# A Mamba-2 layer with a linear side branch: y_diag in channel-major form, split fp32r output projection, x times dt out of PSUM, and new instruction orders

## The chip, the cores and the metric

The kernel runs on one core of a Trainium2 chip. The core has a matmul engine (TensorE, in the profile PE, with its weight loads as PEld), a vector engine (VectorE, DVE), an activation engine (ScalarE, ACT), a general engine (GpSimd, POOL) and SyncE (SP), which issues the DMAs here. SBUF is the on-chip memory, PSUM holds matmul results in eight banks of 512 fp32 columns. The metric is the device time of one execution in microseconds (us). Before the change it is 858.38 us, the median of three runs (854.18 to 859.85).

## The reference

Two sequences of 4096 tokens and 256 features go through one layer. Cut to what matters:

```python
xn = layernorm(x)                                   # no gain or bias
zxbcdt = xn @ W_in                                  # 256 -> 512 z | 768 xBC | 8 dt
z, xBC, dt = split(zxbcdt)
dt = softplus(dt + dt_bias)                         # 8 heads
xBC = silu(causal_conv(xBC, conv_w) + conv_b)       # 4 taps per channel
xs, B, C = split(xBC)                               # 512 | 128 | 128
y = ssd(xs * dt, dt * a, B, C)                      # state-space recurrence, heads of 64
y = (y + xs * D) * silu(z)
y = y * rsqrt(mean(y * y) + EPS) * rms_w
h = xn + y @ W_out
attn = layernorm(h) * ln_g + ln_b
ffn = tanh(xn @ weight @ aux_weight1 @ aux_weight2 + bias)
out = x + attn + ffn
```

The recurrence is computed chunk by chunk: within a chunk, y_diag[l] = sum over s <= l of (C[l].B[s]) exp(A_cum[l] - A_cum[s]) (x dt)[s]; from the chunks before, y_off[l] = exp(A_cum[l]) C[l] . state; then state = decay * state + B^T (x dt weights).

## The kernel before

**Tiling.** A step is a chunk of 128 tokens of both sequences (q = 0, 1), so there are 32 steps. The four engines each run `one_pass(k, b)` for k from -2 to 33, and one pass works on pieces of up to four steps: a pass does the norm statistics of step k+2, the projections of k+1 and k, the recurrence of k and k-1 and the output of k-2. Nothing schedules this at run time: in each engine's `one_pass` the calls stand in the order in which they are issued, and semaphores between the engines hold an instruction until its inputs are there. Buffers of three steps rotate.

**A step on its way.** `norm_stats`, `norm_mean_var` and `norm_apply` (DVE, with a pow on POOL) make xn; `transpose_x` (PE) puts it into a PSUM bank with channels on partitions; ACT's `high_part` rounds it to fp32r and DVE's `low_part` keeps the remainder, so that each projection can be three fp32r products (high x high, high x low, low x high) in place of one fp32 one. `branch_project` makes the side branch and dt in the two banks ring0 and ring1, which ACT's `branch` reads one after the other (tanh, relu, abs); `softplus_exp` (ACT) and then the DVE steps `softplus(k, b, i)` make dt and, as the last one, a_wide = dt * a. These are 11 small instructions (16 columns, the last 64), of which each needs the one before. `conv_project` (six blocks of 128 channels) is followed by `conv_in` (ACT: bias and last tap) and three `tap` instructions of DVE per block, each of which adds to what the tap before wrote. `conv_silu` and `z_silu` (ACT) finish xs and gate.

**The recurrence.** `sums` (PE) makes the cumulated sums of a_wide; ACT copies their rows, DVE's `low_rows` and POOL's `spread_rows` make the operands of one fp32r matmul per four heads, `exponents`, whose result ACT's `decay` takes the exponential of. `b_and_g` makes C.B, `mask_g` (POOL) masks it, `weigh` (DVE) multiplies it with the decays into mm. `x_tokens` transposes xs to tokens on partitions (PE) and ACT copies it to SBUF as xsb; from xsb ACT makes xdt with eight instructions of 64 columns, POOL makes xw (state weights) and xd (skip, x * D). `y_diag` is then eight fp32 matmuls, one per head, with mm[128x128] stationary and xdt of 64 columns moving:

```python
last = mul(yd_bank[:, h * HD:(h + 1) * HD], mm[:, q, h], xdt[:, q, h * HD:(h + 1) * HD], ...)
```

**The output.** `scale_off` (DVE) scales y_off, `add_skip` (POOL) adds xd, `add_diag` and `apply_gate` (DVE) give yg. `square` (ACT) sums its squares, `rms_scale` (POOL, two small instructions per sequence, one of them a pow) makes rr. `transpose_y` and `y_channels` bring yg to channels on partitions, `out_project` is four fp32 matmuls of 256 columns, `last_h` (DVE) applies rr and adds xn. `last_stats`, `last_mean_var`, `last_norm_scale` (POOL, three small instructions per sequence), `last_apply` (ACT) and `output` (POOL) end the step, for each sequence by itself.

**Banks and what follows from them.** yd_bank holds in turn y_diag and the transposed yg of each sequence: `y_diag` of one waits until `y_channels` has read the other's. yoff_bank is shared by `y_off` and `out_project`, xt_bank by `x_tokens` and `states`. A conv or z projection waits until the taps or silu that read its ring bank are through.

## Time and profile before

| | |
|---|---|
| runs, median (lowest to highest) | 858.38 us (854.18 to 859.85) |
| profiled execution | 857.2 us, span 855.5 us |
| granted TensorE clock, mean | 0.976 |
| busy in the span: PE, DVE, POOL, ACT | 800.8, 726.5, 702.0, 681.3 us |
| chain that ended last, largest lines | DVE taps 7%, POOL xw 7%, PE conv and branch products 5% |
| DMA | 19.98 MB, 23 GB/s, hardly busy after the first slice |

The span is the time from the first to the last instruction, and the execution is 1.7 us longer. The first 50 us and the last 55 us are set-up, filling and draining of the pipeline; between them every engine repeats its pass. On PE a matmul in fp32 stands as two records, and PE counts as busy until a modelled end, so its cost is read from start to start. Instructions of DVE and ACT that do not need each other overlap: the next one starts before the last has ended.

### The profile page before, as it was taken

What the parts mean: (1) busy time and instruction counts of PE and PEld (TensorE: products, weight loads), DVE (VectorE), ACT (ScalarE), POOL (GpSimd) and SP (SyncE); (2) the same over time, 40 slices, a digit from 0 to 9 for tenths busy, and PEclk for the clock granted to TensorE, in tenths of its full rate; (3) what the DMA queues carried; (4) which work ended last, traced back from release to release, by engine and by line L of the source; (5) the groups of instructions that cost most, each with busy time, mean ns of one, the idle gap of its engine ahead of it and who ended that gap; (6) DMA issues with size and microseconds to landing.
All of it is one profiled execution on the core that took longest, in us unless ns stands there. A gap on an engine that the chain in (4) does not pass through costs nothing.

```text
span 855.5 us, 18389 instructions
## 1 busy us (share of the span) xinstructions
PE 800.8 (94%) x4944; PEld 671.5 (78%) x4944; DVE 726.5 (85%) x1826; ACT 681.3 (80%) x1767; POOL 702.0 (82%) x1096
## 2 busy tenths in 40 slices
PE   1479999999999999999999999999999999999974
PEld 1368888888888888888888888888888888888753
DVE  1669899998999999899999999999999998998741
ACT  1169888898888888988888889888888898888841
POOL 4036888898888889988888899888888988888884
PEclk9689999999999999999999999999999999999986
DMA  5000000000000000000000000000000000000000
GB/s 174 0 1 13 14 26 26 26 11 14 25 25 25 25 25 25 6 19 25 25 25 25 25 25 1 24 25 25 25 25 25 25 0 24 25 25 13 14 13 25
DMA packets 20848, 19.98 MB, mean 23 GB/s; under 512 B 2646, under 2 KB 20568, under 8 KB 20824
## 3 DMA queue, kind: packets, MB, share of 16 engines
q1 hardware_dynamic: 20824, 19.71, 7.2%
q8 instruction: 10, 0.16, 0.1%
q14 instruction: 14, 0.11, 0.0%
HBM read 11.31 MB, written 8.39 MB: 23 GB/s over the span
## 4 chain that ended last, share of the span: by engine, by line
POOL 39%; DVE 25%; issue 17%; PE 13%; ACT 2%; SPq 2%; POOLq 1%; DVEq 1%; DMA 0%; ACTq 0%
DVE u L624 7%; POOL xw L446 7%; PE ring L1012 5%; POOL obuf L491 4%; POOL left L434 3%; POOL sdec L453 3%; POOL xd L461 3%; POOL rs L483 3%; DVE pa L646 3%; POOL right L430 3%; DVE lay L677 3%; POOL obuf L493 3%; POOL btg L441 2%; DVE lay L683 2%; PE yoff_bank L1149 2%
## 5 line engine op out<-in xcount | busy, mean ns | idle before, releaser
L624 DVE SCALAR_TENSOR_TENSOR u<-ring,cw,u 128x256 f32<-128x256 f32 x576 | 260.5, 469 | 30.4 <-ACT u L847 29.8
L1012 PE MATMUL ring<-xhl,wh 128*128 128x262 f32 x768 | 174.8, 319 | 3.4 <-DVE u L624 3.4
L1012 PE MATMUL ring<-wh,xhl 128*128 128x512 f32 (+1 forms) x512 | 164.1, 374 | 3.3 <-DVE u L624 3.3
L1012 PEld LDWEIGHTS ring<-xhl,wh 128*128 128x128 f32 x768 | 124.7, 193 | 43.6 <-DVE u L624 21.6
L847 ACT ACTIVATE u<-ring,cb,cw 128x256 f32<-128x256 f32 x192 | 107.9, 562 | 45.6 <-PE ring L1012 40.9
L907 ACT ACTIVATE xdt<-xsb,dts 128x64 f32<-128x64 f32 x512 | 128.5, 335 | 0.0
L1131 PE MATMUL yd_bank<-xdt,lay 128*128 128x64 f32 x1024 | 123.2, 274 | 0.9 <-ACT yts L916 0.9
L1149 PE MATMUL yoff_bank<-wo,yts 128*128 128x256 f32 x512 | 122.1, 382 | 1.1 <-ACT yts L916 0.7
L1131 PEld LDWEIGHTS yd_bank<-xdt,lay 128*128 128x128 f32 x1024 | 121.2, 194 | 1.7 <-ACT yts L916 1.3
L1012 PE MATMUL ring<-xhl,wl 128*128 128x262 f32 x384 | 110.2, 287 | 0.0
L1012 PEld LDWEIGHTS ring<-wh,xhl 128*128 128x128 f32 x512 | 93.9, 192 | 20.0 <-issue 7.2
L1149 PEld LDWEIGHTS yoff_bank<-wo,yts 128*128 128x128 f32 x512 | 93.9, 192 | 13.9 <-issue 2.7
L860 ACT ACTIVATE xs<-u 128x512 f32<-128x512 f32 x96 | 60.2, 627 | 45.8 <-DVE u L624 45.5
L677 DVE SCALAR_TENSOR_TENSOR lay<-e_bank,btg 128x512 f32<-128x512 f32 x128 | 86.7, 678 | 1.3 <-POOL btg L441 0.4
L1012 PE MATMUL ring<-wl,xhl 128*128 128x264 f32 (+1 forms) x256 | 87.8, 343 | 0.0
L467 POOL TENSOR_TENSOR lay<-lay,xd 128x512 f32<-128x512 f32 x64 | 81.6, 1276 | 0.0
L891 ACT ACTIVATE e_bank<-e_bank 128x512 f32<-128x512 f32 x128 | 75.4, 590 | 0.3
L1012 PEld LDWEIGHTS ring<-xhl,wl 128*128 128x128 f32 x384 | 73.6, 192 | 0.0
L1112 PE MATMUL yoff_bank<-state,xs 128*128 128x512 f32 x128 | 68.4, 616 | 1.6 <-DVE hh L705 1.3
L491 POOL TENSOR_TENSOR obuf<-hh,lng 128x256 f32<-128x256 f32 x64 | 46.5, 727 | 28.4 <-ACT hh L897 28.4
L705 DVE SCALAR_TENSOR_TENSOR hh<-yoff_bank,rr,xn 128x256 f32<-128x256 f32 x64 | 30.5, 477 | 44.8 <-POOL rr L474 38.4
L1100 PE MATMUL e_bank<-right,left 128*128 128x512 f32 x128 | 66.6, 522 | 1.4 <-POOL left L434 1.4
(134 smaller groups left out, 1995.7 us busy)
## 6 DMA issues: line engine op xcount, KB each, us to landing
xin<-in_x_dram SPq DMA_DIRECT2D x32, 256.0 KB, 2.9
out_dram<-obuf SPq DMA_DIRECT2D x32, 256.0 KB, 2.8
lay<-in_w_in_dram SPq DMA_DIRECT2D x1, 1288.0 KB
wo<-in_w_out_dram SPq DMA_DIRECT2D x1, 512.0 KB
lay<-in_f1t_dram SPq DMA_DIRECT2D x1, 256.0 KB
lay<-in_f2t_dram SPq DMA_DIRECT2D x1, 256.0 KB
lay<-in_f_dram SPq DMA_DIRECT2D x1, 256.0 KB
lng<-in_ln_g_dram SPq DMA_DIRECT2D x1, 128.0 KB
```

Of the source, the lines that this page charges most:

```text
L467: g.tensor_tensor(t2[:, q], t1[:, q], xd[:, q], ALU.add).then_inc(t2_done[q], 1)
L491: g.tensor_tensor(obuf[:, b, q], hh[:, q], lng[:, :], ALU.mult).then_inc(hg_done[q], 1)
L624: v.scalar_tensor_tensor(out=u[:, ct], in0=conv_bank(ct)[:, :, t:t + P], scalar=cw[:, ct, t:t + 1], in1=u[:, ct], op0=ALU.mult, op1=ALU.ad ...
L677: v.scalar_tensor_tensor(out=mm[:, q, hs], in0=e_bank[half][:, :].rearrange("p (j t) -> p j t", t=P), scalar=1.0, in1=btg[:, q, P:2 * P].u ...
L847: s.activation(u[:, ct], conv_bank(ct)[:, :, HALO:PH], ACT.Identity, bias=cb[:, ct:ct + 1], scale=cw[:, ct, HALO:TAPS]).then_inc(u_done[ct ...
L891: s.activation(e_bank[half][:, :], e_bank[half][:, :], ACT.Exp).then_inc(e_done[q][half], 1)
L907: last = s.activation(xdt[:, q, head], xsb[:, q, head], ACT.Copy, scale=dts[:, b, q * H + h:q * H + h + 1])
L1012: last = mul(out, a, c, start=first and i == 0, stop=i == n - 1)
L1100: mul(bank[:, :], left[:, 2 * q + half], right[:, :, :].rearrange("p j t -> p (j t)"), start=True, stop=True)\
L1112: mul(yoff_bank[:, :], xs[:, b, KI + 1, q], state[:, q], start=True, stop=True).then_inc(yoff_in_psum[q], 1)
L1131: last = mul(yd_bank[:, h * HD:(h + 1) * HD], mm[:, q, h], xdt[:, q, h * HD:(h + 1) * HD], start=True, stop=True)
L1149: last = mul(yoff_bank[:, 0:D], yts[:, q, ki], wo[:, ki], start=ki == 0, stop=ki == KI - 1)
```

## The change

1. `LOG_TERMS` goes from 6 to 5: one softplus instruction less per step.
2. ring0 and ring1 become one tensor of two banks, and `branch` reads both with three instructions in place of six.
3. `out_project` uses the three-product form: W_out is split at the start into woh and wol, ACT rounds the transposed yg to fp32r (yts), a new DVE instruction `y_low` keeps the remainder (ytl), and 12 fp32r matmuls take the place of four fp32 ones.
4. `y_diag` is swapped: xdt (64 columns) is stationary, mm (128) moves, the result has channels on partitions, two heads above each other. A new ACT copy `y_copy` takes it to SBUF, `add_skip` adds the skip there (which `skip_x` now makes from xs directly), and a new `y_tokens` transposes it back (4 transposes). `add_diag` adds t1.
5. x times dt is read from PSUM; the copy xsb is gone, xw is made from xdt, and w16 is gone.
6. EPS of the rms norm comes in as a constant 513th column of yg, and `rms_scale`, `last_norm_scale` and `output` do both sequences at once.
7. The four orders are new. `exponents` is one matmul per four heads before and after.

The heart of the diff (orders left out):

```diff
-LOG_TERMS = 6
+LOG_TERMS = 5
...
-        ring0, ring1, e_bank0, e_bank1, xt_bank, bg_bank, yoff_bank, yd_bank = [
+        ring = ctx.enter_context(nc.psum_tensor("ring", [P, 2, 512], F32))
+        ring0, ring1 = ring[:, 0], ring[:, 1]
+        e_bank0, e_bank1, xt_bank, bg_bank, yoff_bank, yd_bank = [
...
-            def scale_x(k, q):
-                pool.wait_ge(xsb_done[q], k + 1)
-                pool.wait_ge(w16_done, k + 1)
-                g.tensor_tensor(heads(xw[:, q]), heads(xsb[:, q]), per_head(w16[:, q * H:(q + 1) * H]), ALU.mult)\
+            def scale_x(k, b, q):
+                pool.wait_ge(xdt_done[q], k + 1)
+                pool.wait_ge(sums_read, k + 1)
+                if begun(k - 1):
+                    pool.wait_ge(st_in_psum[q], k)
+                g.tensor_tensor(heads(xw[:, q]), heads(xdt[:, q]), per_head(exs[:, b, Q * H + q * H:Q * H + (q + 1) * H]), ALU.mult)\
...
             def add_skip(k, q):
-                pool.wait_ge(t1_done[q], k + 1)
+                pool.wait_ge(yc_done[q], k + 1)
                 pool.wait_ge(xd_done[q], k + 1)
-                g.tensor_tensor(t2[:, q], t1[:, q], xd[:, q], ALU.add).then_inc(t2_done[q], 1)
...
+                g.tensor_tensor(yct[:, q], yct[:, q], xd[:, q], ALU.add).then_inc(t2_done[q], 1)
...
+            def rms_scale(k):
+                pool.wait_ge(ss_done[0], k + 1)
+                pool.wait_ge(ss_done[1], k + 1)
...
+                g.tensor_tensor(rr[:, :], ss[:, :], nhalf[:, :], ALU.pow).then_inc(rr_done, 1)
...
+            def output(k, b):
+                pool.wait_ge(hn_done[0], k + 1)
+                pool.wait_ge(hn_done[1], k + 1)
                 pool.wait_ge(stored[b], count16(k, b))
...
+                both = [P, Q, D]
+                g.tensor_tensor(obuf[:, b], hh[:, :, :], lng[:, :].unsqueeze(1).to_broadcast(both), ALU.mult).then_inc(hg_done, 1)
+                pool.wait_ge(hg_done, k + 1)
+                g.tensor_tensor(obuf[:, b], obuf[:, b], res[:, b], ALU.add).then_inc(out_done, 1)
...
             for ki in range(KI):
-                v.tensor_scalar(wo[:, ki], wo[:, ki], rmsw[:, ki:ki + 1], None, ALU.mult)
+                last = v.tensor_scalar(woh[:, ki], wo[:, ki], rmsw[:, ki:ki + 1], None, ALU.mult)
+            last.then_inc(s_sel, 1)
+            dve.wait_ge(s_sel, 11)
+            for ki in range(KI):
+                v.scalar_tensor_tensor(out=wol[:, ki], in0=wo[:, ki], scalar=rmsw[:, ki:ki + 1], in1=woh[:, ki].bitcast(F32),
+                                       op0=ALU.mult, op1=ALU.subtract)
...
+            def y_low(k, q):
+                dve.wait_ge(yts_done[q], k + 1)
+                bank = yd_bank[:, :].rearrange("p (k t) -> p k t", k=KI)
+                v.tensor_tensor(ytl[:, q], bank, yts[:, q].bitcast(F32), ALU.subtract).then_inc(ytl_done[q], 1)
...
-            def branch(k, q):
-                act.wait_ge(f_in_psum[q], k + 1)
-                bank = (ring0, ring1)[q]
+            def branch(k):
+                act.wait_ge(f_in_psum[0], k + 1)
+                act.wait_ge(f_in_psum[1], k + 1)
...
-                    last = s.activation(xdt[:, q, head], xsb[:, q, head], ACT.Copy, scale=dts[:, b, q * H + h:q * H + h + 1])
+                    last = s.activation(xdt[:, q, head], xt_bank[:, head], ACT.Copy, scale=dts[:, b, q * H + h:q * H + h + 1])
...
+            def y_copy(k, q):
+                act.wait_ge(yc_in_psum[q], k + 1)
+                if begun(k - 1):
+                    act.wait_ge(yd_in_psum[q], k)
+                s.activation(yct[:, q], yd_bank[:, :], ACT.Copy).then_inc(yc_done[q], 1)
...
             def y_diag(k, q):
                 if begun(k - 1 + q):
-                    pe.wait_ge(yts_done[1 - q], k + q)
+                    pe.wait_ge(ytl_done[1 - q], k + q)
...
-                    last = mul(yd_bank[:, h * HD:(h + 1) * HD], mm[:, q, h], xdt[:, q, h * HD:(h + 1) * HD],
+                    half = slice(h % 2 * HD, (h % 2 + 1) * HD)
+                    last = mul(yd_bank[half, h // 2 * P:(h // 2 + 1) * P], xdt[:, q, h * HD:(h + 1) * HD], mm[:, q, h],
                                start=True, stop=True)
+                last.then_inc(yc_in_psum[q], 1)
+
+            def y_tokens(k, q):
+                pe.wait_ge(t2_done[q], k + 1)
+                for ki in range(KI):
+                    last = tr(yd_bank[:, ki * P:(ki + 1) * P], yct[:, q, ki * P:(ki + 1) * P], ident[:, :])
                 last.then_inc(yd_in_psum[q], 1)
...
             def out_project(k, q):
-                pe.wait_ge(yts_done[q], k + 1)
+                pe.wait_ge(ytl_done[q], k + 1)
...
+                pairs = []
                 for ki in range(KI):
-                    last = mul(yoff_bank[:, 0:D], yts[:, q, ki], wo[:, ki], start=ki == 0, stop=ki == KI - 1)
+                    pairs += [(yts[:, q, ki], woh[:, ki]), (yts[:, q, ki], wol[:, ki]), (ytl[:, q, ki], woh[:, ki])]
+                last = split_products(yoff_bank[:, 0:D], pairs)
```

**DVE around the softplus steps.** On DVE, before, a stretch in which the first two blocks of taps (L624, u) of step k+1 are done, with the first softplus steps den, rc and sv between them; the ISA and REGISTER_ALU rows only count semaphore values:

```order
L624 SCALAR_TENSOR_TENSOR u<-ring,cw,u 128x256
L637 SCALAR_TENSOR_TENSOR den<-ee 128x16
L623 ISA
L624 SCALAR_TENSOR_TENSOR u<-ring,cw,u 128x256 x2
L623 REGISTER_ALU
L624 SCALAR_TENSOR_TENSOR u<-ring,cw,u 128x256
L635 ISA
L640 RECIPROCAL rc<-den 128x16
L624 SCALAR_TENSOR_TENSOR u<-ring,cw,u 128x256
L635 REGISTER_ALU
L642 TENSOR_TENSOR sv<-ee,rc 128x16
L624 SCALAR_TENSOR_TENSOR u<-ring,cw,u 128x256
```

The same steps in the change, from y_low (L716) and new_state (L702) of step k-1 on:

```order
L716 TENSOR_TENSOR ytl<-yd_bank,yts 128x512
L702 TENSOR_TENSOR state<-xt_bank,sdec 128x512
L649 SCALAR_TENSOR_TENSOR den<-ee 128x16
L647 ISA
L652 RECIPROCAL rc<-den 128x16
L647 REGISTER_ALU
L654 TENSOR_TENSOR sv<-ee,rc 128x16
L647 REGISTER_ALU
L656 TENSOR_TENSOR ww<-sv 128x16
L647 REGISTER_ALU
L658 SCALAR_TENSOR_TENSOR pa<-ww 128x16
L647 REGISTER_ALU
```

They go on without anything between them to a_wide (ten steps in all); the taps, which shared the stretch, follow them, six in a row for blocks 2 and 0 (and as many for blocks 4 and 5 later), each block's three behind each other.

**PE around y_diag of sequence 0.** Before, behind the transposes of xn (L1005) and ahead of sums of the next step (L1069 to L1071):

```order
L1100 MATMUL e_bank<-right,left 128x512
L999 REGISTER_ALU
L1005 MATMUL ring<-ident,xn 128x128 x4
L1131 MATMUL yd_bank<-xdt,lay 128x64 x8
L1069 MATMUL bg_bank<-a_wide,upto 128x16
L1070 MATMUL bg_bank<-a_wide,after 128x16
L1071 MATMUL bg_bank<-upto,a_wide 128x128
```

In the change it stands between two conv projections (L1024), ahead of the transposes of xs (L1093) of the next step and the first products of the output projection of the sequence before:

```order
L1024 MATMUL ring<-xhl,wl 128x262
L1144 MATMUL yd_bank<-lay,xdt 64x128 x8
L1024 MATMUL ring<-xhl,wh 128x262 x2
L1024 MATMUL ring<-xhl,wl 128x262
L1024 MATMUL ring<-xhl,wh 128x262 x2
L1024 MATMUL ring<-xhl,wl 128x262
L1093 MATMUL xt_bank<-ident,xs 128x128 x4
L1024 MATMUL yoff_bank<-woh,yts 128x256
L1024 MATMUL yoff_bank<-wol,yts 128x256
```

Its output is now 64 partitions by 128 columns per head, and it has moved away from sums, which now open PE's pass and wait there for a_wide.

**POOL behind mask_g.** The change's POOL in the middle of its pass: the bias of res (L417), last_norm_scale for both sequences (L487 to L497), add_skip of sequence 1 (L472), the output of both (L504, L506) and scale_x (L450):

```order
L417 TENSOR_TENSOR res<-res,lnb 128x512
L487 TENSOR_SCALAR ve<-mv 128x2
L492 TENSOR_SCALAR shift<-mv 128x2
L494 TENSOR_TENSOR rs<-ve,nhalf 128x2
L497 TENSOR_TENSOR shift<-shift,rs 128x2
L472 TENSOR_TENSOR yct<-yct,xd 128x512
L502 ISA
L504 TENSOR_TENSOR obuf<-hh,lng 128x512
L506 TENSOR_TENSOR obuf<-obuf,res 128x512
L450 TENSOR_TENSOR xw<-xdt,exs 128x512
```

Before, the same place held residual's bias and then sequence 1's own small chain:

```order
L410 TENSOR_TENSOR res<-res,lnb 128x512
L472 TENSOR_SCALAR sse<-ss 128x1
L474 TENSOR_TENSOR rr<-sse,nhalf 128x1
L461 TENSOR_TENSOR xd<-xsb,d_bc 128x512
L467 TENSOR_TENSOR lay<-lay,xd 128x512
L479 TENSOR_SCALAR ve<-mv 128x1
L483 TENSOR_TENSOR rs<-ve,nhalf 128x1
```

The wide output instructions and the add of the skip now stand together, behind a wait for y_copy.

## Rows read from the trace of the kernel before

**Rows 1.** Windows, 400 to 600 us: length, busy us (count) per engine, clock, DMA.

```profile
400.00:600.00 200.00, 199.92 (x1256) 168.01 (x1256) 183.22 (x458) 172.32 (x451) 177.17 (x271) 1.00 0.07 21
```

**Rows 2.** Timeline of DVE (start us, duration us): a_wide of steps 2 and 31.

```profile
98.63 0.22 DVE L659 TENSOR_TENSOR a_wide<-dts,a_neg 128x64 f32<-128x64 f32 x1
...
806.99 0.21 DVE L659 TENSOR_TENSOR a_wide<-dts,a_neg 128x64 f32<-128x64 f32 x1
```

**Rows 3.** Chain that ended last, 795 to 856 us: start, us, records of PE.

```profile
794.94 1.51 PE yoff_bank L1149 x7
...
796.78 1.38 PE ring L1012 x6
...
800.44 0.44 PE xt_bank L1081 x4
800.88 0.73 PE ring L1012 x6
...
827.07 0.86 PE yoff_bank L1112 x2
...
828.17 1.75 PE yd_bank L1131 x16
```

**Rows 4.** Waits: who for whom, us in total, times, longest.

```profile
DVE hh L705 <- POOL rr L474: 38.4, 30, 3.0
```

**Rows 5.** Timeline of DVE: instructions that do not need each other.

```profile
407.17 0.48 DVE L624 SCALAR_TENSOR_TENSOR u<-ring,cw,u 128x256 f32<-128x256 f32 x1
407.56 0.68 DVE L677 SCALAR_TENSOR_TENSOR lay<-e_bank,btg 128x512 f32<-128x512 f32 x1
408.16 0.68 DVE L683 TENSOR_TENSOR lay<-yoff_bank,exs 128x512 f32<-128x512 f32 x1
```

**Rows 6.** Groups by form, ACT: shapes xcount | busy us, mean ns | idle before.

```profile
L879 ACT ACTIVATE xsb<-xt_bank 128x512 f32<-128x512 f32 x64 | 40.0, 625 | 2.2 <-PE xt_bank L1081 2.2
...
L912 ACT ACTIVATE junk<-lay 128x512 f32<-128x512 f32 x64 | 39.5, 617 | 0.4 <-DVE lay L698 0.4
```

**Rows 7.** Timeline of DVE: instructions that need the one before.

```profile
53.96 0.17 DVE L650 SCALAR_TENSOR_TENSOR pb<-pa,sv 128x16 f32<-128x16 f32 x1
54.16 0.17 DVE L653 SCALAR_TENSOR_TENSOR dts<-pb,relu 128x16 f32<-128x16 f32 x1
...
808.68 0.70 DVE L694 TENSOR_TENSOR yd_bank<-yd_bank,lay 128x512 f32<-128x512 f32 x1 [1.48 <-PE yd_bank L1131]
809.42 0.69 DVE L698 TENSOR_TENSOR lay<-yd_bank,gate 128x512 f32<-128x512 f32 x1
```

**Rows 8.** Timeline of all engines, 424 to 450 us: pa on DVE beside POOL.

```profile
433.92 1.27 POOL L410 TENSOR_TENSOR res<-res,lnb 128x512 f32<-128x512 f32 x1
434.27 0.96 DVE L646 SCALAR_TENSOR_TENSOR pa<-pa,ww 128x16 f32<-128x16 f32 x1
...
437.07 1.27 POOL L467 TENSOR_TENSOR lay<-lay,xd 128x512 f32<-128x512 f32 x1
437.45 0.92 DVE L646 SCALAR_TENSOR_TENSOR pa<-pa,ww 128x16 f32<-128x16 f32 x1
```

**Rows 9.** Groups by form, DVE: softplus steps with two SBUF operands.

```profile
L646 DVE SCALAR_TENSOR_TENSOR pa<-pa,ww 128x16 f32<-128x16 f32 x96 | 59.6, 621 | 0.0
...
L659 DVE TENSOR_TENSOR a_wide<-dts,a_neg 128x64 f32<-128x64 f32 x32 | 17.6, 551 | 0.0
L637 DVE SCALAR_TENSOR_TENSOR den<-ee 128x16 f32<-128x16 f32 x32 | 16.1, 504 | 3.1
```

**Rows 10.** Groups by form, POOL: the obuf product, rr's pow and the two-column pow.

```profile
L491 POOL TENSOR_TENSOR obuf<-hh,lng 128x256 f32<-128x256 f32 x64 | 46.5, 727 | 28.4 <-ACT hh L897 28.4
...
L474 POOL TENSOR_TENSOR rr<-sse,nhalf 128x1 f32<-128x1 f32 x64 | 35.0, 546 | 5.3
...
L388 POOL TENSOR_TENSOR rs<-ve,nhalf 128x2 f32<-128x2 f32 x32 | 22.4, 700 | 2.7
```

**Rows 11.** Timeline of DVE in the set-up: the scaling of W_out.

```profile
27.29 1.14 DVE L578 TENSOR_SCALAR wo<-wo,rmsw 128x256 f32<-128x256 f32 x4
```

More of the change, by code:

```diff
@@ L483, in last_norm_scale @@
[L483 to L489 removed]
+                    pool.wait_ge(hn_done[0], k)
+                    pool.wait_ge(hn_done[1], k)
@@ L751, in one_pass @@
                 if live(k):
[L752 to L756 removed]
+                    weigh(k, 0, 1)
                 if live(k - 1):
```

448 lines of the change are left out of this document (215 added, 233 removed).

## The prediction

> **What bounds the kernel now.** First the busy times of a steady stretch, the windows view [rows 1]: PE is busy all the time there, DVE 183 us of 200, ACT 172, POOL 177. Four engines stand near full, so a share says little; what a pass (one step of 128 tokens of both sequences) costs must be counted. The period comes from the instruction that occurs once a step, the write of a_wide: from step 2 to step 31 it moves from 98.63 to 806.99 us [rows 2], 708.4 / 29 = **24.43 us a pass**.
>
> A busy PE is modelled, so I count its pass from start-to-start times in the chain of waits [rows 3]. Six fp32r products of 262 columns take 0.73 us (0.122 each), six of 512 columns 1.38 (0.23), fp32 matmuls stand as two records each: 256 columns 0.216 a record (1.51 / 7), 512 columns 0.43 (0.86 / 2), the 64-column y_diag 0.109 (1.75 / 16), a transpose 0.11 (0.44 / 4). A pass has 36 + 14 products near 262 columns (6.1 us), 12 + 4 fp32r ones of 512 (3.7), 16 records of the output projection (3.5), 32 of y_diag (3.5), 8 fp32 records of 512 (3.4), 22 transposes (2.4) and 10 small records at about 0.11 (1.1): 23.7 us. So **PE sets the period**, with 0.7 us a pass lost to waits. DVE needs 183.22/200 of 24.43 = 22.4 us and is next; 1.3 us of its 2.0 idle is the wait of last_h for rr (38.4 us over 30 passes [rows 4]).
>
> **The change, part by part, per pass.**
>
> *Exponents.* The words say "single exponent matmul", but the kernel before already issues one matmul per half, and this does not change: 0.
>
> *Output projection.* 16 fp32 records of 0.216 (3.5 us) become 24 fp32r products of 256 columns at the 0.122 of the 262-column ones (2.9): PE -0.6. The residual of the activations is a new DVE subtraction of 512 columns out of PSUM for each sequence. A 512-column DVE instruction starts 0.60 after its forerunner [rows 5]: DVE +1.2.
>
> *y_diag swapped.* Still 32 records, now with 64 stationary and 128 moving columns of fp32. A transpose moves 128 columns with 128 stationary in 0.11, the old one 64 moving in 0.109 [rows 3], so moving and loading seem to cost the same there. The two 64-column products of a pair write different halves of the partitions. Bounds: at best each head runs beside its neighbour and the 3.5 us halve, PE -1.7; at worst the load of 64 columns no longer hides behind the stream and adds half of a record's 0.11 to each, PE +1.7, which I hold for unlikely since a load of 128 columns hides in a transpose now. I take 0.11 a record, the nearest row, and keep -1.7 as a rival. The Trainium skill, page "TensorEngine Tiling (Array Packing)", section "Key Properties", says that tiles of the array run loads and matmuls in parallel, but also that changing the tiling mode drains the engine; by the first y_diag would take about half, by the second each of its two visits would pay at both ends. No row here shows either, since all 128 stationary columns are used before.
>
> *New turn through channel-major.* y_tokens adds 8 transposes: PE +0.9. y_copy adds two 512-column ACT copies and removes the two of x_tokens, 625 ns each [rows 6]: ACT 0. The joint branch saves three small ACT instructions. ACT was idle 28 us of 200 [rows 1] and stays hidden behind PE and DVE, as long as these are the fuller ones.
>
> *Sum for PE.* 23.7 - 0.6 + 0.9 = **24.0 us**.
>
> *DVE.* Three things change. (a) +1.2 for y_low, -0.1 for one softplus term. (b) The new order puts dependent instructions next to each other. Independent ones overlap (a tap lasts 0.48, the next instruction starts after 0.39 [rows 5]); where one needs the other's result, the next starts 0.03 to 0.04 after its end: add_diag 808.68 + 0.70, apply_gate 809.42; pb 53.96 + 0.17, dts 54.16 [rows 7]. A tap before its own successor thus costs 0.52 in place of 0.39. Eleven of the 12 such pairs of a pass are now adjacent, where before another instruction stood between: +1.4. add_diag then apply_gate, twice 0.74 for 0.60: +0.3. Ten softplus steps in a row at 0.20 instead of 0.11: +0.8. (c) The softplus steps with two SBUF operands are long when POOL is in a long instruction: pa started at 434.27 under POOL's 433.92 to 435.19 and ended at 435.23; another from 437.45 to 438.37 under POOL's 437.07 to 438.34 [rows 8]. They end with POOL's instruction. The means of 621, 551 and 504 ns [rows 9] against some 0.17 to 0.21 alone [rows 2, 7] come to 3 x 0.45 + 0.34 + 0.33 = 2.0 us a pass of such waiting. If all of it goes: 22.4 + 1.2 - 0.1 + 2.5 - 2.0 = **24.0 us**.
>
> *POOL.* w16 goes (0.2), the pow of rms_scale is done once for both (2 x 546 becomes about 700 ns) and its two sse instructions go, last_norm_scale likewise, and obuf is written in 2 x 1.28 (two full operands of 512 columns, as in [rows 8]) in place of 4 x 0.727 [rows 10]: about -2. Not on the path: POOL has the slack, and its late results (rr, shift2) are what count. rr now waits for the squares of both sequences. Between apply_gate of sequence 1 and last_h of sequence 0 stand five taps and a small pair, 2.5 us; the square (0.62 [rows 6], and 0.2 for the readout of its sum), the pow (0.7 [rows 10]) and hops of 0.3 need 1.8. It just fits, and behind last_h stand y_off on PE and then scale_off.
>
> *The loop.* a_done (end of softplus) now releases sums at PE's start of pass, and PE goes from there in one piece to the branch products; ACT then does branch, y_channels and square (three of 512 columns, 0.6 each), the square's readout, relu, vabs, b_and_g and softplus_exp (together about 2.9 us, an estimate) before the ten softplus steps (2.1 us). PE up to the branch is 18.5 us (24.0 less what stands behind it: y_diag 1.75, two conv projections 1.46, states 0.86, eight transposes 0.88, b_and_g and one exponents 0.55), so this loop alone is 23.5 plus every wait in it: no room against a period of 24.
>
> *Ends.* The set-up has four more DVE instructions where four took 1.14 us on the way to the first step [rows 11]: +1.2. The drain gets y_copy (0.6), add_skip (1.28, formerly beside y_diag), four transposes (0.44) and y_low (0.7) in its chain, +3.0, and norms both sequences in one chain of wider instructions in place of two behind each other, which I put at -1.7. Together +2.5.
>
> **Forecast.** Two engines now need 24.0 us, where one needed 23.7 and the other 22.4. With the old 0.7 of lost time the period is 24.7; since DVE and PE have no slack towards each other any more and one softplus step in a pass probably still meets a POOL instruction, I add 0.3: 25.0 us. 30 passes x 0.57 = +17, ends +2.5: span 855.5 -> 875; the profiled execution lay 1.7 above its span (857.2) and 1.2 under the median of the runs (858.38): **877 us**, 2% slower.
>
> **Rivals.**
> 1. *The sides of the array overlap and the orders fit* (20%). y_diag falls to half, PE to 22.3, and DVE with 24.0 and hardly a wait sets the period: 24.0 x 30 gives -13, ends +2.5: 846 us. For it: POOL is freer, and the wait for rr goes. Against it: DVE would have to be busy 99% of the time, where PE before managed 97%. It decides if DVE idles less than 0.3 us a pass.
> 2. *It balances* (18%). Period 24.3 to 24.5: 857 to 863 us.
> 3. *The softplus run collides with POOL* (17%). Nine of its ten steps have two SBUF operands, and they come right after new_state. POOL's order there is last_norm_scale, then add_skip of sequence 1 (waiting for y_copy), then the two obuf instructions and scale_x. If y_copy is early (the case in which y_diag is fast), add_skip of 1.28 us and the obuf pair fall on the last steps. Each blocked step waits for a whole POOL instruction: one or two a pass, 1.2 to 2.4 us straight in the loop above, period 25.7 to 27: 898 to 935 us. It decides from one full collision in each pass.
> 4. *The forecast* (45%): 24.6 to 25.5, 866 to 893 us.
>
> A measurement of this kernel tells about 1% from no change. Faster by over 1%: 0.20 (rival 1); within 1%: 0.18; slower: 0.62. The range takes the forecast, rival 2, the slow part of rival 1 and the lower end of 3: **849 to 903 us**.
>
> **What the profile after would show.** The period between two a_wide writes (25.0 forecast). y_diag's start-to-start: 0.11 a record, or 0.055 to 0.08 if the halves overlap. The projection: 1.45 us a sequence. Neighbouring taps 0.52 apart. The softplus run 2.1 us long; over 3 us means rival 3, with a POOL instruction ending where a step ends. DVE above 95% busy or in dependency gaps in steady state. Wrong would be: DVE idle by over 2 us a pass at waits for PE or ACT (then the order, not the load, sets the time), or records of y_diag above 0.15.

## The result: 964.66 us, 12.6% slower

Median of the changed kernel 964.66 us (963.63 to 966.43, 4 runs), of the kernel before 856.77 (854.18 to 859.85, 4 runs): ratio **1.126, 95% interval 1.1213 to 1.1307**. The forecast was 877 us, the range 849 to 903. All of it lies outside.

| | before | after |
|---|---|---|
| profiled span | 855.5 us | 963.7 us |
| mean granted clock of TensorE | 0.976 | 0.953 |
| write of a_wide, step 2 to step 31 | 98.63 to 806.99: 24.43 us a pass | 86.39 to 901.19: 28.10 us a pass |
| first write of a_wide; span after the last | 54.37; 48.5 us | 42.47; 62.5 us |

First the period and a steady stretch: the timeline (start us, duration us) of the writes of a_wide in steps 0, 2 and 31, and the windows view (busy us and count per engine, clock, DMA).

```profile
42.47 0.22 DVE L671 TENSOR_TENSOR a_wide<-dts,a_neg 128x64 f32<-128x64 f32 x1
86.39 0.23 DVE L671 TENSOR_TENSOR a_wide<-dts,a_neg 128x64 f32<-128x64 f32 x1
...
901.19 1.24 DVE L671 TENSOR_TENSOR a_wide<-dts,a_neg 128x64 f32<-128x64 f32 x1
```

```profile
400.00:600.00 200.00, 176.56 (x1202) 144.92 (x1201) 185.60 (x407) 147.76 (x369) 140.60 (x178) 0.96 0.06 18
```

Against [rows 1] PE fell from 199.9 to 176.6 busy, ACT from 172 to 148 and POOL from 177 to 141, and the granted clock from 1.00 to 0.96. Only DVE stayed about where it was (183.2 before, 185.6 after). The same instruction, the write of a_wide, took 0.22 us in step 0 and 1.24 in step 31. The groups by form (shapes xcount | busy us, mean ns | idle before) say which DVE instructions grew:

```profile
L620 DVE TENSOR_SCALAR xn<-xin,mv,rs 128x256 f32<-128x256 f32 x64 | 54.4, 888 | 3.2 <-POOL rs L397 1.4
...
L665 DVE SCALAR_TENSOR_TENSOR dts<-pb,relu 128x16 f32<-128x16 f32 x32 | 36.6, 1144 | 1.1
L671 DVE TENSOR_TENSOR a_wide<-dts,a_neg 128x64 f32<-128x64 f32 x32 | 35.5, 1109 | 1.1
...
L658 DVE SCALAR_TENSOR_TENSOR pa<-pa,ww 128x16 f32<-128x16 f32 x64 | 11.2, 175 | 2.2
```

Two operations of 16 and 64 columns take 1.1 us each in the mean, while pa, with the same kind of operands and a few places earlier in the run, takes 0.175. What stands beside them is in the timeline of all engines:

```profile
501.55 0.51 PE L1024 MATMUL ring<-xhl,wh 128*128 128x262 f32 x2
501.67 0.60 ACT L929 ACTIVATE yct<-yd_bank 128x512 f32<-128x512 f32 x1 [0.47 <-PE yd_bank L1144]
...
502.23 0.18 DVE L662 SCALAR_TENSOR_TENSOR pb<-pa,sv 128x16 f32<-128x16 f32 x1
...
502.34 1.27 POOL L472 TENSOR_TENSOR yct<-yct,xd 128x512 f32<-128x512 f32 x1 [2.34 <-ACT yct L929]
502.38 0.60 PE L1093 MATMUL xt_bank<-ident,xs 128*128 128x128 f32 x4
502.44 1.20 DVE L665 SCALAR_TENSOR_TENSOR dts<-pb,relu 128x16 f32<-128x16 f32 x1
...
503.57 1.27 POOL L504 TENSOR_TENSOR obuf<-hh,lng 128x512 f32<-128x512 f32 x1
503.68 1.24 DVE L671 TENSOR_TENSOR a_wide<-dts,a_neg 128x64 f32<-128x64 f32 x1
...
504.97 0.28 PE L1081 MATMUL bg_bank<-a_wide,upto 128*128 128x16 f32 x1 [1.98 <-DVE a_wide L671]
```

Read it by ends. dts starts at 502.44, 0.10 after POOL's add_skip, and ends at 503.64, 0.03 after POOL's end (503.61). a_wide starts at 503.68, 0.11 after the obuf product, and ends at 504.92 against POOL's 504.84. PE has nothing to do from 502.98 on and stands until a_wide is there, 1.98 us. The step dts is longer than 1 us in 30 of the 32 passes, a_wide in 28, and the rows of waits (who for whom, us in total, times, longest) add PE's pause up to about 2 us a pass:

```profile
PEld bg_bank L1081 <- DVE a_wide L671: 67.3, 32, 2.4
PE bg_bank L1081 <- DVE a_wide L671: 59.7, 32, 2.2
PEld ring L1017 <- DVE xn L620: 49.6, 31, 1.6
```

The last row is a second case. The two norm_apply of a pass fell beside two POOL instructions of 1.05 and 1.09 us:

```profile
520.08 1.05 POOL L450 TENSOR_TENSOR xw<-xdt,exs 128x512 f32<-128x512 f32 x1 [0.37 <-ACT xdt L916]
...
520.38 1.94 DVE L620 TENSOR_SCALAR xn<-xin,mv,rs 128x256 f32<-128x256 f32 x2
...
521.09 1.09 POOL L457 TENSOR_TENSOR sdec<-state,exs 128x512 f32<-128x512 f32 x1
...
522.38 0.33 PE L1017 MATMUL ring<-ident,xn 128*128 128x128 f32 x1 [1.19 <-DVE xn L620]
```

norm_apply has one SBUF tensor operand only, and yet two took 1.94 us, where in the kernel before each of the 64 lasted between 396 and 413 ns. The third thing is the clock. The mean period is 28.10, but the median pass lasts 27.46: the rest, 0.6 us a pass, are passes with a stretch of 3.4 us, or twice that, at half of the full clock (1.2 in place of 2.4 GHz). Eleven such stretches lie between 100 and 800 us. In them the products of the output projection start 0.21 us apart, at full clock 0.115:

```profile
508.00:511.00 3.00, 3.00 (x16) 3.00 (x16) 2.90 (x7) 1.47 (x6) 0.31 (x1) 0.53 0.00 0
```

```profile
508.13 0.41 PE L1024 MATMUL yoff_bank<-wol,yts 128*128 128x256 f32 x1
508.34 0.41 PE L1024 MATMUL yoff_bank<-woh,ytl 128*128 128x256 f32 x1
...
518.16 0.28 PE L1024 MATMUL yoff_bank<-wol,yts 128*128 128x256 f32 x1
518.27 0.28 PE L1024 MATMUL yoff_bank<-woh,ytl 128*128 128x256 f32 x1
```

What went well is y_diag. Its 16 records of a visit start at 500.53 and the next product at 501.55: 1.02 us, **0.064 a record against 0.109** in [rows 3]. Within a visit they come in pairs: the two records of a pair start 0.007 us apart, and a new pair starts every 0.11 us, so a pair now costs what one record did. The change is not free at its edge: the product in front of a visit holds PE for 0.21 us (500.32 to 500.53), the same kind of product in front of fp32 transposes for 0.12 (502.26 to 502.38).

```profile
500.32 0.28 PE L1024 MATMUL ring<-xhl,wl 128*128 128x262 f32 x1
500.53 1.09 PE L1144 MATMUL yd_bank<-lay,xdt 128*64 128x128 f32 x16
...
502.26 0.29 PE L1024 MATMUL ring<-xhl,wl 128*128 128x262 f32 x1
```

### The profile page after: what moved, and what is told of

It is laid out like the page before. It is cut to its first block and busy times, and to the rows that moved or that the text cites. A ratio compares the mean times of both kernels' runs of the same rounds, so it can differ in the third digit from the quotient of the medians.

```text
span 963.7 us, 19087 instructions
## 1 busy us (share of the span) xinstructions
PE 806.3 (84%) x5456; PEld 658.0 (68%) x5456; DVE 845.0 (88%) x1862; ACT 670.8 (70%) x1673; POOL 644.2 (67%) x841
## 5 line engine op out<-in xcount | busy, mean ns | idle before, releaser
L1024 PE MATMUL ring<-xhl,wh 128*128 128x262 f32 x768 | 178.1, 324 | 8.6 <-DVE u L636 7.2
L1024 PEld LDWEIGHTS ring<-xhl,wh 128*128 128x128 f32 x768 | 129.4, 200 | 53.8 <-issue 28.9
L1024 PE MATMUL ring<-wh,xhl 128*128 128x512 f32 (+1 forms) x512 | 150.9, 347 | 1.4 <-DVE u L636 1.3
L472 POOL TENSOR_TENSOR yct<-yct,xd 128x512 f32<-128x512 f32 x64 | 82.1, 1282 | 77.6 <-ACT yct L929 77.6
L1024 PE MATMUL ring<-xhl,wl 128*128 128x262 f32 x384 | 112.4, 293 | 0.0
L916 ACT ACTIVATE xdt<-xt_bank,dts 128x64 f32<-128x64 f32 x512 | 111.6, 337 | 0.3 <-PE xt_bank L1093 0.3
L1024 PEld LDWEIGHTS ring<-wh,xhl 128*128 128x128 f32 x512 | 93.2, 190 | 17.9 <-DVE u L636 6.3
L481 POOL TENSOR_TENSOR rr<-ss,nhalf 128x2 f32<-128x2 f32 x32 | 22.5, 702 | 102.2 <-issue 101.7
L1024 PE MATMUL ring<-wl,xhl 128*128 128x264 f32 (+1 forms) x256 | 87.6, 342 | 0.0
L1024 PE MATMUL yoff_bank<-woh,yts 128*128 128x256 f32 x256 | 83.6, 326 | 1.4 <-DVE ytl L716 1.4
L450 POOL TENSOR_TENSOR xw<-xdt,exs 128x512 f32<-128x512 f32 x64 | 67.0, 1046 | 15.0 <-ACT xdt L916 14.1
L1024 PE MATMUL yoff_bank<-wol,yts 128*128 128x256 f32 x256 | 77.0, 301 | 0.0
L1024 PE MATMUL yoff_bank<-woh,ytl 128*128 128x256 f32 x256 | 76.3, 298 | 0.0
L1024 PEld LDWEIGHTS ring<-xhl,wl 128*128 128x128 f32 x384 | 76.1, 198 | 0.0
L466 POOL TENSOR_TENSOR xd<-xs,d_ch 128x512 f32<-128x512 f32 x64 | 66.7, 1042 | 8.5 <-ACT xs L872 4.3
L1144 PE MATMUL yd_bank<-lay,xdt 128*64 128x128 f32 x1024 | 70.7, 281 | 1.8 <-DVE ytl L716 1.8
L457 POOL TENSOR_TENSOR sdec<-state,exs 128x512 f32<-128x512 f32 x64 | 68.3, 1067 | 0.0
```

The lines of the kernel that those rows point to most:

```text
L450: g.tensor_tensor(heads(xw[:, q]), heads(xdt[:, q]), per_head(exs[:, b, Q * H + q * H:Q * H + (q + 1) * H]), ALU.mult)\
L457: g.tensor_tensor(heads(sdec[:, q]), heads(state[:, q]), per_head(exs[:, b, 2 * Q * H + q * H:2 * Q * H + (q + 1) * H]), ALU.mult)\
L466: g.tensor_tensor(xd[:, q].rearrange("p (c t) -> p c t", c=KI), xs[:, b, 0:KI, q], d_ch[:, :].unsqueeze(2).to_broadcast([P, KI, P]), ALU.m ...
L472: g.tensor_tensor(yct[:, q], yct[:, q], xd[:, q], ALU.add).then_inc(t2_done[q], 1)
L916: last = s.activation(xdt[:, q, head], xt_bank[:, head], ACT.Copy, scale=dts[:, b, q * H + h:q * H + h + 1])
L1024: last = mul(out, a, c, start=first and i == 0, stop=i == n - 1)
```

## The experiments

Each is timed against the kernel before on the same chip (medians 856.0 to 858.8 us there). The ratio is the time divided by that of the kernel before; the last two columns are the mean durations of dts, a_wide and one norm_apply.

| run | us | ratio, 95% | us a pass | softplus: dts, a_wide ns | xn ns |
|---|---|---|---|---|---|
| changed kernel | 964.7 | 1.126 [1.121, 1.131] | 28.10 | 1144, 1109 | 888 |
| e1 softplus operands in PSUM | 885.6 | 1.034 [1.031, 1.036] | 25.44 | 174, 220 | 815 |
| e2 norm_apply with a PSUM operand | 957.2 | 1.117 [1.114, 1.120] | 27.82 | 1141, 1108 | 478 |
| e3 both | 871.1 | 1.017 [1.014, 1.020] | 24.96 | 174, 220 | 477 |
| e4 y_diag on one half of the columns | 916.4 | 1.069 [1.067, 1.072] | 26.27 | 175, 225 | 975 |
| e8 softplus run earlier | 951.9 | 1.108 [1.104, 1.112] | 27.68 | 174, 224 | 835 |
| e6 = e3, dependent neighbours apart | 907.8 | 1.058 [1.055, 1.061] | 26.13 | 174, 220 | 478 |
| e7 = e3, y_low of 4 columns | 845.4 | 0.986 [0.983, 0.989] | 24.15 | 174, 221 | 478 |
| e9 = e1, norm_apply on ACT | 876.3 | 1.021 [1.020, 1.023] | 25.10 | 174, 220 | on ACT |
| e10 = e9, one place later | 876.9 | 1.022 [1.019, 1.024] | 25.07 | 174, 220 | on ACT |
| e11 = e9, norm_stats ahead of low_part | 1110.2 | 1.295 [1.293, 1.298] | 32.93 | 174, 220 | on ACT |
| e12 = e9, add_diag ahead of low_part | 870.8 | 1.014 [1.012, 1.017] | 24.90 | 174, 220 | on ACT |
| e13 = e12, last_h earlier | 857.2 | 1.001 [1.000, 1.003] | 24.41 | 174, 221 | on ACT |

**e1: the softplus run without its second SBUF operand.** The theory: DVE waits for POOL's running instruction when both of its operands come from SBUF. The rival: the run is slow for its place behind new_state, or PE's wait only moves. pb and the negated a are kept in unused columns of a PSUM bank; the same ten instructions at the same places.

```diff
-v.tensor_scalar(a_neg[:, :], a_neg[:, :], -1.0, None, ALU.mult)
+v.tensor_scalar(bg_bank[:, 288:288 + Q * H], a_neg[:, :], -1.0, None, ALU.mult)
-ins = v.scalar_tensor_tensor(out=pb[:, :], in0=pa[:, :], ...
+ins = v.scalar_tensor_tensor(out=bg_bank[:, 256:256 + Q * H], in0=pa[:, :], ...
```

> The changed kernel with pb and the negated a_log kept in PSUM, so that the last two softplus steps (dts, a_wide) have one SBUF operand each and need not share anything with POOL. Theory A (these two wait for POOL's add_skip and output instructions, and stand in the loop a_done, sums, PE, branch, softplus): dts and a_wide fall from 1.14 and 1.11 us to about 0.2 each, the period of an undisturbed pass from 27.4 to 25.5 us; PE's wait for a_wide (2 us a pass) goes and with it most of the stretches at half clock: about 885 us. Rival B (PE, ACT and the order bound the pass, the waiting fills time that would be idle anyway): under 0.5 us a pass, over 945 us. Rival C (the TensorE clock is the cause): the short instructions change nothing by themselves, 940 to 965 us.

885.6 us: theory A, within a microsecond. The groups by form:

```profile
L671 DVE TENSOR_TENSOR a_wide<-dts,bg_bank 128x64 f32<-128x64 f32 x32 | 7.0, 220 | 1.1
L665 DVE SCALAR_TENSOR_TENSOR dts<-bg_bank,relu 128x16 f32<-128x16 f32 x32 | 5.6, 174 | 1.1
```

The place of one operand in each of two instructions is worth 79 us. 2.0 us a pass are the collision itself (27.46 to 25.4 by the medians), the other 0.6 the half-clock stretches, of which none is left between 100 and 800 us. Left to itself, in e1, the run ends only about 0.54 us after add_skip's start: this small overlap had cost 2 us a pass, since each of the last two steps waited for a whole POOL instruction.

**e2: norm_apply with its scale in PSUM.** rs is copied into two columns of PSUM and norm_apply becomes a scalar_tensor_tensor, of which only xin lies in SBUF as a tensor.

```diff
+v.tensor_scalar(bg_bank[:, 320:322], rs1[:, :], 1.0, None, ALU.mult)
-v.tensor_scalar(xn[:, b, q], xin[:, b, q], mv1[:, q, 0:1], rs1[:, q:q + 1], ALU.subtract, ALU.mult)
+v.scalar_tensor_tensor(out=xn[:, b, q], in0=xin[:, b, q], scalar=mv1[:, q, 0:1],
+                       in1=bg_bank[:, 320 + q:321 + q].to_broadcast([P, D]), op0=ALU.subtract, op1=ALU.mult)
```

> The changed kernel with norm_apply as scalar_tensor_tensor whose second operand, rs, lies in PSUM (one small copy more). Theory A: the two instructions of norm_apply, 888 ns each on the mean against 400 before, wait for POOL's xw and sdec; now 0.48 each, and transpose_x comes 1 us earlier: about -1.1 us a pass, 925 to 935 us. Rival B: no change, over 955 us.

xn fell to 478 ns. But with the 2 us pause at a_wide left in, 27 of the 29 passes now had a half-clock stretch: granted clock 0.93 in the window, mean period 27.82. The two passes without one, at the start, took 25.85 and 25.88 us, where the changed kernel's same two took 26.39 and 26.42: half a microsecond less a pass at full clock, as e1 to e3 show later.

```profile
L625 DVE SCALAR_TENSOR_TENSOR xn<-xin,mv,bg_bank 128x256 f32<-128x256 f32 x64 | 27.9, 478 | 1.1
```

```profile
400.00:600.00 200.00, 182.85 (x1232) 152.57 (x1231) 183.59 (x418) 150.64 (x372) 142.61 (x182) 0.93 0.06 18
```

The miss (expected 925 to 935) teaches that the pause can be paid again through the clock, and that shortening another part of the pass helps little as long as the pause stays. Why e2, whose PE pauses less in all than that of the changed kernel, had 24 such stretches to its 11 stays open. The instruction changed its form along with the place of its operand, so e2 does not say which of the two ended the wait.

**e3: both.**

> Both edits. Theory A: the waits add up: -2.0, -1.1 and the lost clock of some 0.7 us a pass: 845 to 865 us, about the time of the kernel before. Rival B: no better than the larger single one; the next bound is near, above 880 us. Rival C: the clock alone gives 20 us: 940 us.

871.1 us, six above the expected range, 24.96 us a pass. This is the changed kernel without collisions, and its period is the one that the forecast had (25.0). Against e1 norm_apply is worth 0.48 us a pass.

**e4: y_diag without the two column halves.** All heads write the same 64 partitions (half of y is lost).

```diff
+v.memset(yd_bank[:, :], 0.0)
-half = slice(h % 2 * HD, (h % 2 + 1) * HD)
+half = slice(0, HD)
```

> The changed kernel with all eight heads of y_diag written to partitions 0 to 63, so that no two neighbours lie in different column halves of the array (half of y is lost in this kernel). If the 0.064 us a record of the changed kernel comes from neighbours running side by side, y_diag goes back to about 0.11 a record, 1.75 us a visit instead of 1.02, and the time rises by 0 to 0.75 us a pass (only one of the two visits stands in the loop): 964 to 988 us. If it comes from the shorter stationary load alone, y_diag stays at 1.02 us and the time at 964.

The first part came: from the first record of a visit to the next product it is 1.89 us in place of 1.02 (busy 1.96 in place of 1.09), and the records start 0.109 apart. So the shorter stationary side alone gains nothing, and the pairs need different halves. (In e4 both heads of a pair also write the same cells; it does not tell the same half from the same cells.) The second was wrong in sign: with a slower y_diag the kernel is 48 us **faster**, since y_copy comes later, add_skip with it, and the softplus run is over by then, in this stretch 0.33 us before add_skip starts:

```profile
505.42 1.96 PE L1145 MATMUL yd_bank<-lay,xdt 128*64 128x128 f32 x16
...
507.54 0.23 DVE L672 TENSOR_TENSOR a_wide<-dts,a_neg 128x64 f32<-128x64 f32 x1
...
508.10 1.28 POOL L472 TENSOR_TENSOR yct<-yct,xd 128x512 f32<-128x512 f32 x1 [3.22 <-ACT yct L930]
```

```profile
L672 DVE TENSOR_TENSOR a_wide<-dts,a_neg 128x64 f32<-128x64 f32 x32 | 7.2, 225 | 1.1
L666 DVE SCALAR_TENSOR_TENSOR dts<-pb,relu 128x16 f32<-128x16 f32 x32 | 5.6, 175 | 1.1
```

**e8: only the order.** The softplus run stands ahead of y_low(k-1,0) and new_state(k-1,1).

```diff
-                    y_low(k - 1, 0)
-                    new_state(k - 1, 1)
 ...                 softplus(k + 1, b1, 0) to softplus(k + 1, b1, 9)
+                    y_low(k - 1, 0)
+                    new_state(k - 1, 1)
```

> The changed kernel, no PSUM edit; in VectorE's order the softplus run stands ahead of y_low(k-1,0) and new_state(k-1,1) instead of behind them, so dts and a_wide come 1.5 to 1.9 us earlier against GpSimd's add_skip. Theory A, the collision is a matter of where the run ends against the start of add_skip (502.3 us in the stretch read): both stand free before it, about 2.05 us a pass less and the half-clock stretches gone: period 25.2 to 25.8 us, 878 to 900 us; norm_apply still waits (0.8 to 0.9 us an instruction). Theory B, y_low comes later and TensorE waits for ytl in place of a_wide: period 26.5 us or more, 920 to 965 us. Theory C, add_skip moves earlier with it (y_copy waits for TensorE, which waits for a_wide) and the collision comes back in part: dts or a_wide at a mean of 0.5 us or more, 905 to 945 us.

The collision is gone (a_wide 224 ns) by order alone, but only 13 us are won: theory B. PE now waits for ytl, 2.4 us a pass, and half-clock stretches stay. So a place in the order can hide the collision, but this stretch of DVE's order has no room: what comes first delays the other.

```profile
PEld yd_bank L1145 <- DVE ytl L716: 83.5, 33, 2.9
PE yd_bank L1145 <- DVE ytl L716: 75.3, 32, 2.7
```

**e6 and e7: what bounds the rest, on top of e3.** e6 puts an independent instruction between dependent neighbours (calls only, shortened):

```diff
-tap(k, 5, 1); tap(k, 5, 2); last_h(k - 2, b1, 1)
+tap(k, 5, 1); last_h(k - 2, b1, 1); tap(k, 5, 2)
-tap(2,0) tap(2,1) tap(2,2) tap(0,0) tap(0,1) tap(0,2) norm_stats
+tap(2,0) tap(0,0) tap(2,1) tap(0,1) tap(2,2) norm_stats tap(0,2)
...
```

> The changed kernel with both PSUM edits (softplus and norm_apply free of VectorE's waits for GpSimd; 871.1 us, 24.96 us a pass) and VectorE's order changed: thirteen or so pairs of dependent neighbours (taps of one tile, add_diag and apply_gate, last_h among them) get an independent instruction between them. Theory A, VectorE's instruction stream is the bound that is left: each separated pair saves some 0.12 us (0.51 to 0.39 behind a tap), 1.3 to 1.7 us a pass: period 23.3 to 23.8 us, 820 to 838 us, faster than the kernel before. Theory B, the bound that is left is TensorE (192 busy of 200 us) and the waits between it and its partners: the period moves by 0.4 us or less, 857 to 873 us, and the freed time of VectorE turns up as its waits. Theory C, an order that delays a late result (apply_gate, last_h): slower than 873 us.

37 us slower than e3: theory C. DVE is busy 174 of 200 us where it was 187; what it saves, it waits. Two results come later in this order. The banks of the conv tiles come free later, and the loads of PE wait for them nearly twice as long, then ACT and DVE for PE. And PE stands 0.9 us a pass in front of the transposes of xs until DVE's new state is there, which it did not in e3:

```profile
PEld ring L1031 <- DVE u L642: 64.9, 69, 1.5
...
DVE hh L729 <- PE yoff_bank L1031: 28.8, 30, 1.0
PE xt_bank L1100 <- DVE state L708: 27.9, 31, 0.9
```

In e3 the first of these is 36.3. So e6 speaks against this order, not against every order that separates neighbours. e7 keeps the order and computes 4 of each tile's 128 columns in y_low (the rest of ytl is set to 0 once, so most of the low part of y is left out of the projection):

```diff
-v.tensor_tensor(ytl[:, q], bank, yts[:, q].bitcast(F32), ALU.subtract)
+v.tensor_tensor(ytl[:, q, :, 0:4], bank[:, :, 0:4], yts[:, q, :, 0:4].bitcast(F32), ALU.subtract)
```

> The changed kernel with both PSUM edits, and y_low computes 4 of each tile's 128 columns (the rest of ytl stays 0 from the start; TensorE's twelve products stay): the low part of the output projection is left out of the result, its cost to VectorE nearly so. Theory A, VectorE's stream bounds the pass: 2 x (0.685 - 0.15) = 1.1 us less, period 23.9 us, 834 to 842 us: then the 1.2 us a pass that the forecast put on y_low was a price really paid. Theory B, TensorE and its chain bound it: 0.4 us a pass or less, 857 to 871 us.

1.03 us less DVE work gives 0.81 us a pass: in e3 DVE's stream lies on the path, and y_low costs 0.81 of the 1.2 us that the forecast put on it. Whether the load of DVE counts, or the moment at which last_h and xn come, e7 does not tell; e9 does. PE is at 197 of 200 there.

```profile
400.00:600.00 200.00, 196.85 (x1402) 160.75 (x1402) 186.80 (x482) 171.20 (x432) 164.31 (x208) 1.00 0.06 21
```

**e9 to e13: norm_apply on ACT.** Since a real kernel can't drop y_low, DVE is relieved in another way, with everything computed: its busy time falls from 23.35 us a pass in e3 to 22.27.

```diff
+g.tensor_scalar(shift1[:, :], mv1[:, :, 0], -1.0, None, ALU.mult)           # POOL
+g.tensor_tensor(shift1[:, :], shift1[:, :], rs1[:, :], ALU.mult)
+s.activation(xn[:, b, q], xin[:, b, q], ACT.Identity, bias=shift1[:, q:q + 1], scale=rs1[:, q:q + 1])
```

> The changed kernel with the softplus operands in PSUM, and norm_apply taken off VectorE: ScalarE computes xn as Identity with scale rs and bias -mean x rs (GpSimd makes the bias with two small operations), ahead of conv_silu(k+1,2). Everything is computed. Against the variant with both PSUM edits (24.96 us a pass) VectorE loses 2 x 0.48 us, the 0.16 us copy of rs and about 0.2 us of gaps: 1.3 us; ScalarE gains 2 x 0.4 us to 166 of 200. Theory A, VectorE's stream bounded that variant (the shortened y_low took 1.03 us off it and 0.81 us off the pass) and TensorE comes next at about 23.9 us: period 23.9 to 24.3 us, 836 to 852 us, faster than the kernel before. Theory B, ScalarE is late with xn or with what stands behind it (conv_silu, z_silu, high_part): period 24.7 us or more, 862 us or more.

> As the kernel before it, with norm_apply on ScalarE one place later, behind conv_silu(k+1,2). Theory A (VectorE's load was the bound): place matters by less than 0.3 us a pass, 836 to 856 us. Theory B (the transposes wait for xn, as TensorE already did in the changed kernel for L620): xn comes 0.6 us or more later and the period is up by as much, 855 to 875 us.

e9 missed (theory B): 25.10 us a pass with DVE at 177 of 200, so less load on DVE alone gains nothing. By the waits, the chain last_h, xn (which takes the buffer that last_h reads), transposes, high_part, low_part is now what ends last. e10 missed both its theories: moving xn by one place changes nothing (25.07), since conv_silu then only fills the time in which ACT stood waiting for last_h. In the stretches read xn starts 0.11 us after last_h's end in e9 and 0.24 in e10.

```profile
DVE xhl L625 <- ACT xhl L848: 61.6, 32, 5.1
...
PE ring L1025 <- ACT xn L842: 33.3, 32, 12.1
...
ACT xn L842 <- DVE hh L721: 22.6, 29, 0.8
```

e11 fills DVE's wait of 1.8 us with other work, norm_stats(k+2) among it.

```diff
+                    last_stats(k - 2, 0); last_mean_var(k - 2, 0)
+                    norm_stats(k + 2, b2)
                     low_part(k + 1, b1)
```

> The kernel with norm_apply on ScalarE (25.10 us a pass), in which VectorE stood 1.8 us in every pass in front of low_part, waiting for high_part. In VectorE's order last_stats(k-2,0), last_mean_var(k-2,0) and norm_stats(k+2) (0.42 + 0.18 + 0.83 us) now stand ahead of low_part and fill that wait. Everything is computed. Theory A, VectorE's stream with this wait in it was the bound: 1.2 to 1.4 us a pass less as far as TensorE (192.2 busy of 200 us, 24.1 us a pass) allows: period 24.0 to 24.4 us, 838 to 853 us, faster than the kernel before. Theory B, the chain hh, xn, transposes, high_part, low_part is the bound by itself: the wait shrinks, another one grows, period 24.8 us or more, 866 us or more.

The worst of all: norm_stats(k+2) needs a load that SP issues only after residual_bias(k-1) on POOL, in the same pass. DVE stood for it 7.6 us a pass, and low_part and PE behind it. PE's pause was 6.7 us a pass, and the clock paid again: 21 half-clock stretches of 6.8 or 10.2 us between 100 and 800 us.

```profile
DVE st L610 <- DMA xin<-in_x_dram: 219.3, 29, 8.6
```

e12 has add_diag(k-1,0) there in its place, which waits for no load.

```diff
+                    last_stats(k - 2, 0); last_mean_var(k - 2, 0)
+                    add_diag(k - 1, 0)
                     low_part(k + 1, b1)
                     apply_gate(k - 1, bo, 0)
```

> The kernel with norm_apply on ScalarE (876 us, 25.10 us a pass); ahead of low_part, where VectorE stood 1.8 us a pass, now come last_stats(k-2,0), last_mean_var(k-2,0) and add_diag(k-1,0) (0.42 + 0.18 + 0.72 us), none of which waits for a load; yd_bank, which add_diag reads, is full at 507.0 us in that kernel's stretch, 0.5 us before low_part began at 507.5. Everything is computed. Theory A, VectorE's stream with the wait in it is the bound: 0.7 to 1.2 us a pass less, as far as TensorE (24.1 us busy a pass) allows: period 24.1 to 24.5 us, 842 to 857 us. Theory B, low_part comes 0.3 us or more later for add_diag and TensorE waits for it in the z part: period 24.8 us or more, 864 us or more.

24.90 us, in theory B's range but not by its mechanism: PE does not wait longer for low_part. add_diag now waits for PE (30.7 us in 32 passes), which itself stands 0.7 us a pass in front of the transposes of xn, as in e9. e13 goes at that pause: last_h between the last two taps.

```diff
                     tap(k, 5, 1)
-                    tap(k, 5, 2)
                     last_h(k - 2, b1, 1)
+                    tap(k, 5, 2)
```

> The kernel with norm_apply on ScalarE and add_diag ahead of low_part (870.8 us, 24.90 us a pass). Its TensorE is busy 192.3 of 200 us and has one long pause a pass, 0.71 us in front of the transposes of xn; xn waits for last_h(k-2,1), which ends at 475.75 in the stretch read, and the output projection that last_h reads ends at 474.68. Here last_h stands between tap(k,5,1) and tap(k,5,2) in place of behind them. Everything is computed. Theory A, that pause closes by as much as last_h comes earlier, 0.4 to 0.5 us a pass: period 24.35 to 24.55 us, 852 to 862 us, no difference from the kernel before. Theory B, TensorE then waits elsewhere (ring for the sixth conv tile's taps, yd_bank): period 24.75 us or more, 865 us or more.

857.2 us, 24.41 a pass, both inside theory A. One instruction moved by one place gave 0.49 us a pass (13.6 us by the medians, of which up to 2.8 may lie in the chip: the kernel before was that much faster beside e13 than beside e12). PE's pause is 0.23 us, and PE is busy 196 of 200:

```profile
469.07 0.66 PE L1026 MATMUL ring<-ident,xn 128*128 128x128 f32 x4 [0.23 <-ACT xn L843]
```

```profile
400.00:600.00 200.00, 196.31 (x1402) 159.14 (x1401) 182.85 (x454) 175.16 (x445) 162.65 (x222) 1.00 0.08 24
```

With both collisions and this pause away the changed kernel is level with the kernel before, 1.001 [1.000, 1.003]. No variant that computes everything beats it. The comparison may flatter the change: the kernel before, which has collisions of its own ([rows 9]), did not get PSUM operands.

## Why the prediction was wrong

The step that failed is in the DVE sum: "(c) ... If all of it goes: 22.4 + 1.2 - 0.1 + 2.5 - **2.0** = 24.0", together with the 0.3 in the forecast for "one softplus step in a pass". It let 2.0 us of contention go; the trace has two full collisions in nearly every pass, the run of ten steps lasts 4.2 us in place of 2.1, and PE waits 2 us for it. With them taken out (e1, e3) the period is 24.96 us, the forecast's 25.0. The step beside it, "Not on the path: POOL has the slack", failed in the same way: POOL was weighed by its load, and what counted was when its long instructions start. The mechanism was named, as rival 3, with 17%. Point by point:

- **Rival 3** described the place (add_skip, then the obuf product, on the last steps), the size of one case (a whole POOL instruction) and the loop: 25.7 to 27 us. Measured: two steps, and 2.0 us a pass (e1), which takes 25.4 to the median of 27.46; with the clock 28.10, 965 us, beyond this rival's 935 too. Its condition, "if y_copy is early (the case in which y_diag is fast)", is what e4 shows. The error was to hold the rival as less likely than the forecast without looking where POOL would be: add_skip waits 2.3 us for y_copy in the rows of the result, so POOL starts whenever y_copy ends, and without the collision the ten steps last 2.2 us.
- **Rivals 1 and 3 hung together.** The fast y_diag was priced as a gain in one case and as a condition in the other. Both happened; the prediction gave the first 846 us, and e4 shows that the slow y_diag would have been 48 us better here.
- **norm_apply was not in the sum.** Here one tensor operand in SBUF was enough for a wait: 401 ns became 888. Before, it stood beside POOL's one-column operations (the pow of last_norm_scale in 58 of 64 cases), after, beside xw and sdec of 1.05 and 1.09 us, and each ends 0.15 us after them. Once the softplus operands were out of the way this was worth 0.48 us a pass (e1 to e3), half of its own 0.97. The Trainium skill, page "GPSIMD Engine Reference", section "Specifications", says that GpSimd shares its SBUF interfaces with VectorE and that contention comes with DVE instructions in a 2-port performance mode or with two SBUF inputs. The trace agrees for dts and a_wide (two inputs, 0.17 to 1.14 us and 0.22 to 1.11), and e1 agrees in that a PSUM operand ends it; that norm_apply ran in such a mode no row says by name.
- **The clock** was in no step. With a pause of 2 us of PE in each pass came 11 stretches at 1.2 GHz between 100 and 800 us, 0.6 us a pass in the changed kernel; e2 had 24 of them, which took back about half of its gain of 0.5, e8 (2.4 us in each pass) 10. In e1, e3, e4, e7, e9, e10, e12 and e13, where the longest pause that comes back in each pass is 1.2 us or less, there is none, and in e6 (two of 0.9 us a pass) one.
- **y_diag** was mis-sized: 0.064 a record, 2.05 us a pass in place of 3.5. Of the two claims of the Trainium skill, page "TensorEngine Tiling (Array Packing)", section "Key Properties", the trace agrees with the first (tiles work in parallel, and e4 ends it); for the drain when the mode changes, 1.02 against 0.87 us (half of 16 x 0.109) leaves 0.15 us a visit, and the product in front of a visit takes 0.09 us more than elsewhere (0.21 against 0.12, in e4 too). These are the places where a drain would show; that it is one no run says.
- **The projection** was right: 12 products from 517.95 on start 0.115 apart, 0.122 forecast. **Adjacent taps** too: 2.94 us for six, (2.94 - 0.48) / 5 = 0.49 to 0.51 each, 0.52 forecast. The one order that spread them (e6) was slower, since banks and the new state came later; that the price of adjacency can't be had back by another order is not shown. **y_low** 1.03 us of work for 0.81 a pass (e7). **Ends** +2.1 us (42.47 + 62.5 against 54.37 + 48.5), +2.5 forecast.
- **The base** of the forecast, 25.0 us a pass without collisions, is e3's 24.96; 877 us stands between e3's 871 and e1's 886. That it agrees is partly luck: PE's sum of 24.0 held the slow y_diag (1.45 us too much), and e13's pass of 24.41 us is longer than the rest of the sum, 22.55, by 1.9 us, of which 0.5 are visible pauses. The 1.4 left were priced at nothing. Half of them were in the kernel before already: the prediction called the 0.7 us between its sum and its period lost to waits, but PE is busy 199.92 of 200 us in [rows 1]. The trace shows where part of such time goes: the first fp32r product behind fp32 ones holds PE for about 0.2 us in place of 0.12, and so does the one in front of y_diag. The rest stays open, and so does what the kernel before would gain from the PSUM operands, which wasn't tried.
- **Sums.** The forecast's own terms (855.5 + 17 + 2.5 + 1.7 + 1.2) come to 878 in place of 877, rival 1's to 848 in place of 846. Nothing hangs on it.
